# Attention: the six maximum tiles at other places among the ten exponent tiles

## The reference

```
q = (x @ Wq), 16 heads of 8;  k = (x @ Wk), v = (x @ Wv), 4 key heads of 8   (rope on q and k)
att = softmax(causal(q k^T) / sqrt(8))        # 512 x 512 for each of 16 heads, 16 batches
x = x + (att @ v) @ Wo
```

## Time and profile before

| | us |
|---|---|
| Median of 3 runs (lowest, highest) | 1874.82 (1872.78, 1875.02) |
| The profiled execution's own time | 1875.22 |
| Its span, first to last instruction | 1873.2 |
| PE, PEld busy | 1581.5, 1107.9 |
| DVE, ACT, POOL busy | 1360.9, 1089.0, 760.4 |
| Mean granted clock of TensorE (1 = 2.4 GHz) | 0.915 |

### The profile page before, as it was taken

One profiled execution on the slowest core, in us unless ns is written; L12 is line 12 of the kernel. 1 busy time (PEld: TensorE's weight loads), 2 busy tenths in 40 slices (PEclk: granted clock), 3 DMA queues, 4 the chain that ended last, 5 costly groups with the idle time before them and its releaser, 6 DMA issues. The chain is left out here.

```text
span 1873.2 us, 39185 instructions
## 1 busy us (share of the span) xinstructions
PE 1581.5 (84%) x11698; PEld 1107.9 (59%) x11698; DVE 1360.9 (73%) x3422; ACT 1089.0 (58%) x2225; POOL 760.4 (41%) x1170
## 2 busy tenths in 40 slices
PE   4878749999999999998699529999977751999998
PEld 1444424555555555554355329999964531999997
DVE  4898746777777777774388668777768976777776
ACT  2444313666666666666466427787755531877876
POOL 1565542333333333333233256665401212666540
PEclk9989856999999999999899759999988875999999
DMA  5111231111111111110011301111000110121110
GB/s 135 31 38 50 59 105 36 43 43 42 41 41 41 44 39 42 40 35 2 1 34 33 110 19 39 38 34 29 25 1 23 34 34 12 39 60 46 43 48 23
DMA packets 72819, 76.39 MB, mean 41 GB/s; under 512 B 13040, under 2 KB 61488, under 8 KB 72752
## 3 DMA queue, kind: packets, MB, share of 16 engines
q1 hardware_dynamic: 64560, 58.77, 10.9%
q0 software_dynamic: 8192, 16.79, 3.4%
HBM read 51.40 MB, written 24.12 MB: 40 GB/s over the span
## 5 line engine op out<-in xcount | busy, mean ns | idle before, releaser
L951 DVE TENSOR_REDUCE at_negmax<-at_s_ps 128x2 f32<-128x1024 f32 (+3 forms) x384 | 394.5, 1045 | 174.9 <-PE at_s_ps L741 170.4
L862 ACT ACTIVATE at_p<-at_x_ps 128x512 f32<-128x512 f32 x640 | 353.5, 591 | 224.1 <-PE at_x_ps L751 221.3
L918 POOL TENSOR_SCALAR_AFFINE_SELECT at_p<-at_p 128x256 f32<-128x256 f32 (+1 forms) x448 | 190.7, 438 | 354.9 <-ACT at_p L862 354.9
L1175 POOL DMA_INDIRECT e_x_in<-xn,e_row_c x256 | 258.5, 1010 | 145.7 <-POOL e_row_c L1171 103.5
L739 PE MATMUL at_s_ps<-at_kr,at_qr 72*128 72x512 bf16 (+3 forms) x1024 | 253.0, 312 | 20.6 <-DMA at_kr<-k_parts 18.2
L751 PE MATMUL at_x_ps<-at_qr,at_kr 74*128 74x512 bf16 (+3 forms) x1024 | 236.4, 306 | 23.0 <-ACT at_p L862 12.9
L1296 DVE TENSOR_TENSOR e_hid_lo<-e_hid,e_hid_hi 128x512 fp32r<-128x512 f32 x256 | 177.2, 693 | 85.3 <-ACT e_hid_hi L1260 85.3
L741 PE MATMUL at_s_ps<-maskb,identb 128*128 128x128 bf16 x1024 | 202.1, 225 | 0.0
L1259 ACT ACTIVATE e_hid<-e_h_ps 128x512 f32<-128x512 f32 x256 | 155.0, 605 | 39.4 <-PE e_h_ps L1201 38.9
L766 PE MATMUL at_o_ps<-at_p,at_va 128*32 128x512 f32 (+3 forms) x2048 | 157.0, 449 | 1.6 <-POOL at_p L918 1.6
L1201 PE MATMUL e_h_ps<-e_x_hi,w_hi 128*128 128x256 f32 x512 | 156.0, 305 | 0.1
(11 more groups left out here) (184 smaller groups left out, 3515.2 us busy)
## 6 DMA issues: line engine op xcount, KB each, us to landing
at_qr<-q_parts SPq DMA_DIRECT2D x192, 96.0 KB
k_parts<-m_kparts SPq DMA_DIRECT2D x48, 96.0 KB
at_kr<-k_parts SPq DMA_DIRECT2D x64, 72.0 KB
xres<-in_x_dram SPq DMA_DIRECT2D x8, 512.0 KB, 7.3
xn<-m_n_xhat SPq DMA_DIRECT2D x16, 256.0 KB, 2.3
e_x_in<-xn,e_row_c POOLq DMA_INDIRECT x256, 2.5
xn<-sc_n_xhat SPq DMA_DIRECT2D x16, 256.0 KB, 2.3
out_dram<-xres SPq DMA_DIRECT2D x16, 256.0 KB, 2.3
```

The lines of the kernel that those rows point to most:

```text
L862: a.activation(p_sb[g % 2][:, i, :], x_ps[i % 2][:], ACT.Exp, scale=SCALE).then_inc(x_read, 1)
L918: sel = gp.affine_select(out=part, in_=part, compare_op=ALU.is_ge, fill=0.0, base=0, pattern=[[0, n] for n in part.shape[1:-1]] + [[1, P]] ...
L951: v.tensor_reduce(negmax[u][:, h0:h0 + len(heads), c], s_ps[k % 2][:, 0:len(heads) * pitch].rearrange("p (j w) -> p j w", w=pitch)[:, :, 0:w],
L1175: nc.gpsimd.indirect_dma_start(out=x_in[k][u][:], out_offset=None, in_=xn_dram, in_offset=bass.IndirectOffsetOnAxis(ap=row_c[k][:, u:u + 1 ...
```

## The change

The table `S_BEFORE` says before which exponent tile each maximum tile is made. Five of its six entries are changed or moved; nothing else.

```diff
-S_BEFORE = {0: 0, 2: 1, 3: 2, 5: 3, 7: 4, 8: 5}
+S_BEFORE = {0: 0, 1: 1, 5: 2, 6: 3, 8: 4, 9: 5}
```

## The result

The changed kernel takes 1889.82 us (median of 4 runs, 1889.03 to 1892.07) against 1873.98 us of the kernel before on the same chip: a ratio of 1.0087 with a 95% interval of 1.0069 to 1.0104. It is slower, by 0.9%. The forecast was 1888, in a range of 1879 to 1897.

What follows compares the result with a forecast made beforehand. Attention was taken as bound by a chain passing between TensorE and ScalarE, with VectorE slack. M0's new wait outweighed the gains: +0.89 us a batch, +12.5 over 14, +0.6 elsewhere, +13.1 together, giving 1888 us, range 1879 to 1897.

Steps and rivals of the forecast that it cites:

- E3 directly behind V: Start of each interval: exponent tile E3 starts at 0 and not 0.46 us after the value products V; ScalarE gains 0.46.
- E7 waits for E5's exponential: Exponent tile E7, without M4 in front: stall of 0.70 us for g even, 0.23 for g odd.
- M0 waits 0.56 us for M4's reduction: Maximum tile M0 reuses M4's buffer: 0.91 us of work between them against 1.47 needed, so 0.56 wait in every interval.
- M1 covers E1's wait, E2's stays: Next step's tiles: M1 in front of E1 hides its wait; E2 may start 1.05 us after E0, tiles take 1.00.
- The clock holds: TensorE in attention: clock stays at full speed; the opposing rival, one fall a batch, gave 1919 us, chance 0.07.
- The rule cited from the Trainium skill: Transpose T behind E7: transposes do not count as busy for the clock gate as matmuls do, so T prolongs the idle stretch.
- The rivals: Three alternatives to the forecast: M0 does not wait (chance 0.08), nothing changes (0.08), the clock falls (0.07).
- A kernel bound by the issue of its own instructions: TensorE's whole stream: same instructions in another order take the same time, 1875 us; chance 0.08.
- one whose M0 does not wait: M0 of every step: buffer released in time, each interval 0.56 us shorter than forecast, 36.01 a batch, total 1855; chance 0.08.
- The sum: V to V: start of M4 + 6.35 us; batch 38.25 against 37.36, +0.89, 14 batches +12.5; together with the rest +13.1.
- The rest: Attention outside the 14 batches: first batch's full-clock intervals +0.6 us in all; last interval with maximum tiles even; first groups 0.
- The last groups, which I took as even: End of attention: the last interval with maximum tiles, to the step without any, comes out even, as M0 is not there.

Runs made afterwards that it cites:

- E9: Not a follow-up run: an exponent tile on TensorE, issued after M5 and before the next step's M0 in the changed kernel; it has no measured kernel time.

## Why the prediction was right

- **E3 directly behind V, a gain of 0.46 us for ScalarE.** Right: its idle time is 1.83 where it was 2.46. I had said 2.02; the other 0.2 is work of ScalarE that ends later beside V.
- **E7 waits for E5's exponential, to 2.65 us after V for g even.** Right: 2.66. T ended and M4 began at 3.33 (3.32 forecast).
- **M0 waits 0.56 us for M4's reduction, in every interval.** Right: 0.57, and shown from two sides, by work put between the two tiles and by a shorter reduction. This is the step that decides the sign.
- **M1 covers E1's wait, E2's stays.** Right in outcome, since E1 does not wait; but the run with M1 moved back shows that M0's wait alone does this. As a credit to M1 the step was wrong, as a time it was not.
- **The clock holds.** Right, 1.00 from 340 to 860 us. The rule cited from the Trainium skill, "TensorE: Matmul & The Clock Gate", Part 4: PE-mode transpose, made no difference here: E7's wait of 0.68 us and T's 0.44 stand close together, and the clock stayed.
- **The rivals.** A kernel bound by the issue of its own instructions would have kept 37.36 us a batch, and one whose M0 does not wait would have taken 36.01; it took 38.50, with the clock at 1.00.
- **The sum.** An interval was (start of M4) + 6.35; it is 6.41 (9.74 less 3.33). M0 to E0 takes 0.57 and not 0.55, E0 to E2 1.07 and not 1.05, and 0.01 each lies in M4 to M0 and E2 to V. That makes the batch 38.50 and not 38.25, 3 us over the 12 batches of the loop. The terms that were too small are these handovers, each off by 0.01 or 0.02 us only, but used 59 times.
- **The rest.** The batches behind the loop cost 1.68 us more each and not 0.89, 1.6 us for the two that are whole. The first three intervals cost 0.9 (28.65 before, 29.54 after) where I had 0.6. The last groups, which I took as even, came out 1.2 us shorter (35.82 to 34.64 us from the last V of g = 0 to the last V), with a granted clock of 0.95 and not 0.90. From the first V to the last the profiled executions differ by 16.8 us. The layers behind attention took some 2.8 us less in the execution of the changed kernel: their first expert product stands 16.6 us later and the last 13.8. Of this 1.7 us lie where the first expert layer ends and the scan layer begins. The same instructions take 16.78 us there in the kernel before (1389.40 to 1406.18), with a granted clock of 0.57, and 15.05 in the changed kernel (1405.72 to 1420.77), with 0.81. Nothing in my sum speaks of that, and whether it belongs to the order or to the single execution is open.

The sum of 13.1 us thus met 15.8, by medians. The mechanism was right and the attention layer cost more than my sum, 16.8 us; that the total came within 2 us of the forecast owes something to luck, as the layers behind took less in the profiled execution.

The last four intervals of the layer are a term that my sum put at nothing and that moves by several us. Over the profiled executions of all the kernels here they take 33.0 to 39.0 us, the shortest at a mean granted clock of 0.98 and the longest at 0.82. One execution of each kernel was profiled, so the runs don't tell whether a kernel always gets the same clock there.

## What to carry to other kernels

With two buffers, tile k+2 is not late because of its own place but because of tile k's: count the work between the two, and compare it with the time from the end of the first to the release of its buffer (here 0.91 us of work against 1.48). Read both numbers as moments in one timeline, not as lengths: I missed M4's wait for M2 by doing otherwise. And a wait that a move covers is worth something only as long as no other wait in the same chain covers it already.

The order `{0: 0, 1: 1, 5: 2, 6: 3, 7: 4, 9: 5}`, one entry away from the changed kernel, takes 1847 us, 1.6% less than the kernel before.

## What the runs showed of the hardware

In batches written out behind the loop a tile that really stalls starts later than the same tile in the loop. Of the changed kernel behind the loop:

```profile
806.05 0.27 PE L739 MATMUL at_s_ps<-at_kr,at_qr 72*128 72x256 bf16 x1
...
808.30 0.38 PE L739 MATMUL at_s_ps<-at_kr,at_qr 72*128 72x512 bf16 x1 [0.50 <-DVE at_negmax L951]
```

M0 comes 2.25 us after M4 (806.05 to 808.30) and not 2.16, and ScalarE's exponential 0.47 us after E0 (808.86 to 809.33) and not 0.41. Both have two waits in front of them, one of them long fulfilled. Moving the fulfilled wait one tile ahead took 0.08 us out of each interval. That ScalarE's half has the same cause was not tried.

The kernel before has the same delay, and it doesn't show in the length of its batches. There E0, which also has two waits in front of it, waits a little for ScalarE. It starts 7.61 us after V in the loop (486.90 to 494.51) and 7.70 behind it (823.15 to 830.85):

```profile
494.51 0.88 PE L751 MATMUL at_x_ps<-at_qr,at_kr 74*128 74x512 bf16 x2
```
```profile
830.85 0.79 PE L751 MATMUL at_x_ps<-at_qr,at_kr 74*128 74x512 bf16 x2
```

M1 comes 8.32 us after V in both, as E1 stands between them and waits for E9's exponential in either case. With M1 alone moved, M1 stands in front of E1 and covers that wait. There E0 starts at 7.61 and 7.69 us after V, and the interval is 9.14 us long behind the loop and 9.00 in it.
